# Folding two key chunks of one query tile per half head by a relu of their score difference

## The reference

```
q = x @ W_q + b_q;  k = x @ W_k + b_k;  v = x @ W_v + b_v
q = q @ W_s
scores = jnp.einsum('bhqd,bhkd->bhqk', q, k) / jnp.sqrt(jnp.float32(Hd))
attn = jax.nn.softmax(scores, axis=-1)
out = jnp.einsum('bhqk,bhkd->bhqd', attn, v)
```

## Time and profile before

| | |
|---|---|
| median of 3 runs | 1736.55 us (1734.66 to 1736.87) |
| profiled execution, its span | 1734.7 us |
| weighing in the attention loop, first to last start | 139.2 to 1397.7 us |
| PE, DVE, ACT, POOL busy | 97%, 87%, 74%, 13% |
| one unit in the steady loop | 19.64 us |

### The profile page before, as it was taken

How to read it: one execution, slowest core, us unless ns; L and a number is a source line. 1 busy time by engine, 2 the same in 40 slices (tenths; PEclk the granted TensorE clock), 3 DMA queues, 4 the chain that set the end, 5 groups by cost and what they waited for, 6 DMA issues and landing times. The chain is left out here.

```text
span 1734.7 us, 43731 instructions
## 1 busy us (share of the span) xinstructions
PE 1685.5 (97%) x17251; PEld 969.8 (56%) x17251; DVE 1513.5 (87%) x1908; ACT 1291.7 (74%) x2454; POOL 229.3 (13%) x300
## 2 busy tenths in 40 slices
PE   8999999999999999999999999999999998599998
PEld 5645555555555555555555554555555586488887
DVE  5678999999999999999999999999999476687774
ACT  2327888888888888888888888888888834365663
POOL 0422012100010000001000000100000012135433
PEclk9999999999999999999999999999999997599999
DMA  8660443222222223323222223342220331235332
GB/s 265 207 178 24 92 98 53 41 41 39 52 55 39 41 49 52 47 40 65 41 42 39 39 41 54 59 60 39 41 42 12 108 107 61 98 101 143 89 82 37
DMA packets 93658, 122.03 MB, mean 70 GB/s; under 512 B 24060, under 2 KB 70716, under 8 KB 90348
## 3 DMA queue, kind: packets, MB, share of 16 engines
q1 hardware_dynamic: 84492, 109.22, 28.1%
q0 software_dynamic: 6144, 8.39, 2.7%
q10 hardware_dynamic: 2816, 1.61, 0.3%
HBM read 79.35 MB, written 38.54 MB: 68 GB/s over the span
## 5 line engine op out<-in xcount | busy, mean ns | idle before, releaser
L230 DVE TENSOR_REDUCE pmax<-ps 128x2 f32<-128x1024 f32 x1024 | 1191.6, 1215 | 54.2 <-PE ps L223 50.2
L1080 ACT ACTIVATE pt<-ps 128x512 f32<-128x512 f32 x2048 | 1079.4, 600 | 179.8 <-PE ps L584 157.7
L223 PE MATMUL ps<-kp,qp 48*128 48x512 f32 x2048 | 622.4, 458 | 2.9 <-DVE pmax L230 2.9
L1139 PE MATMUL ps<-pt,v_st 128*32 128x256 f32 (+1 forms) x10752 | 589.7, 334 | 0.7 <-ACT pt L1080 0.7
L584 PE MATMUL ps<-qp,kp 50*128 50x512 f32 x2048 | 560.8, 422 | 0.5 <-ACT pt L1080 0.5
L584 PEld LDWEIGHTS ps<-qp,kp 50*128 50x128 f32 x2048 | 292.5, 185 | 265.2 <-ACT pt L1080 263.1
L1139 PEld LDWEIGHTS ps<-pt,v_st 128*32 128x32 f32 x10752 | 265.7, 109 | 261.0 <-issue 187.2
L223 PEld LDWEIGHTS ps<-kp,qp 48*128 48x128 f32 x2048 | 245.6, 184 | 108.1 <-issue 89.8
L213 POOL CAST m_parts<-rowmax_t 128x32 fp32r<-128x32 f32 x64 | 13.5, 211 | 864.5 <-DVE rowmax_t L247 864.5
L1752 PE MATMUL ps<-w_l,hid_h 128*128 128x256 f32 x256 | 72.3, 283 | 0.0
L446 ACT ACTIVATE pt<-ps,xb 128x512 fp32r<-128x512 f32 x32 | 21.8, 687 | 64.7 <-PE ps L613 63.7
(11 more groups left out here) (229 smaller groups left out, 1297.6 us busy)
## 6 DMA issues: line engine op xcount, KB each, us to landing
kp<-k_parts SPq DMA_DIRECT2D x186, 128.0 KB, 4.5
v_all<-L_ffn_w SPq DMA_DIRECT2D x16, 1024.0 KB, 6.9
qp<-q_parts SPq DMA_DIRECT2D x186, 64.0 KB, 4.1
k_parts<-pt SPq DMA_DIRECT2D x16, 512.0 KB, 3.4
q_parts<-pt SPq DMA_DIRECT2D x16, 512.0 KB, 2.9
o_rows<-o_sb SPq DMA_DIRECT2D x64, 128.0 KB, 3.4
sums_c<-o_rows SPq DMA_DIRECT2D x512, 0.5 KB
m_rows<-m_parts SPq DMA_DIRECT2D x256, 2.0 KB
```

Of the source, the lines that this page charges most:

```text
L223: last = nc.tensor.matmul(slot[:, half * CH:(half + 1) * CH], qp[rows, r, a * P:(a + 1) * P], kp[rows, r, c * CH:(c + 1) * CH], start=True ...
L230: v.reduce_max(pmax[:, u % 2, 2 * k:2 * k + 2], slot.rearrange("p (f t) -> p f t", f=2), AX.X).then_inc(groups_out, 1)
L1080: nc.scalar.activation(pt[:, s % PTS, half * CH:(half + 1) * CH], bank(n % SCORE_BANKS), ACT.Exp, scale=SCALE).then_inc(scores_out, 1)
L1139: last = mm(acc[32 * j:32 * (j + 1), first * QB:(first + many) * QB], v_st[:, h % NBUF, kt, :], probs[:, :, j * QB:(j + 1) * QB], start=kt ...
```

## The change

For 60 of the 64 units (2 to 61) two of the 16 groups are computed in another way. The fourth pair of tiles (FOLD_TILE = 3) has four key chunks; of those, 2 and 3 (groups k = 14 and 15) are folded: max(a, b) = b + relu(a - b).

- POOL makes a negated copy `q_minus` of the 128 queries (two operations, behind the split of the maxima of the unit before).
- PE computes q·k2 - q·k3 in the score ring, in the unit before, ahead of its chunk 6: for both halves one matmul with `qp` and then one with `q_minus` into the same bank. The two difference chunks take two successive places of the ring, so a unit now uses 34 of them.
- ACT takes the relu of both difference chunks from PSUM to `fold` (128 x 1024 in SBUF), between the exponentials of chunks 5 and 6.
- Group k = 14 is no longer filled or reduced. Group k = 15 is filled as before, and DVE adds `fold` to it and takes the maximum in one operation per half.
- One block per unit (b == 5, from unit 1 on) fills one group where it filled two. The order of the other groups and chunks stays.
- Counts on `scores_out`, `scores_full` and `groups_out` follow the new numbering.

The diff, cut to its core:

```diff
+FOLD_TILE, FOLD_FROM, FOLD_END = KT // NCH - 1, 2, UNITS - 2
+FOLD_K = FOLD_TILE * NCH + NCH - 1
+FOLD_PLACE = 6
+GROUPS = [(u, k) for u in range(UNITS) for k in range(KT) if not (folds(u) and k == FOLD_K - 1)]
+FOLD_BEFORE = {(u - 1) * UNIT_CHUNKS + FOLD_PLACE: u for u in range(FOLD_FROM, FOLD_END)}
+RING, FOLD_RING = [], {}
+for chunk in range(UNITS * UNIT_CHUNKS):
+    if chunk in FOLD_BEFORE:
+        for half in range(2):
+            FOLD_RING[FOLD_BEFORE[chunk], half] = len(RING) + len(FOLD_RING)
+    RING.append(len(RING) + len(FOLD_RING))
...
         def reduce_group(dve, v, n, slot):
-            u, k = divmod(n, KT)
+            u, k = GROUPS[n]
             dve.wait_ge(groups_full, n + 1)
-            v.reduce_max(pmax[:, u % 2, 2 * k:2 * k + 2], slot.rearrange("p (f t) -> p f t", f=2),
-                         AX.X).then_inc(groups_out, 1)
+            if folds(u) and k == FOLD_K:
+                if u < FOLD_FROM + 2:
+                    v.memset(pmax[:, u % 2, 2 * k - 2:2 * k], LOWEST)
+                for half in range(2):
+                    dve.wait_ge(scores_out, FOLD_RING[u, half] + 1)
+                    last = v.tensor_tensor_reduce(fold[:, half, :], slot[:, half * CH:(half + 1) * CH], fold[:, half, :],
+                                                  1.0, LOWEST, ALU.add, ALU.max,
+                                                  accum_out=pmax[:, u % 2, 2 * k + half:2 * k + half + 1])
+                last.then_inc(groups_out, 1)
+            else:
+                v.reduce_max(pmax[:, u % 2, 2 * k:2 * k + 2], slot.rearrange("p (f t) -> p f t", f=2),
+                             AX.X).then_inc(groups_out, 1)
...
+        def fold_scores(pe, u):
+            h, f = divmod(u, HALVES)
+            a = f * (QT // 2) + FOLD_TILE
+            pe.wait_ge(q_negated, u - FOLD_FROM + 1)
+            for half in range(2):
+                at, rows = FOLD_RING[u, half], slice(HALF * half, HALF * half + KROWS)
+                pe.wait_ge(scores_out, at - SCORE_BANKS + 1)
+                nc.tensor.matmul(ring_bank(at), qp[rows, h % NBUF, a * P:(a + 1) * P],
+                                 kp[rows, h % NBUF, 2 * CH:3 * CH], start=True, stop=False)
+            for half in range(2):
+                at, rows = FOLD_RING[u, half], slice(HALF * half, HALF * half + KROWS)
+                nc.tensor.matmul(ring_bank(at), q_minus[rows, :],
+                                 kp[rows, h % NBUF, 3 * CH:4 * CH], start=False, stop=True).then_inc(scores_full, 1)
+
+        def negate_queries(pool, g, u):
...
+            for half in range(2):
+                rows = slice(HALF * half, HALF * half + KROWS)
+                links["pool"](g.tensor_scalar(q_minus[rows, :], qp[rows, r, a * P:(a + 1) * P].bitcast(F32), -1.0, None, ALU.mult))
+            pool.sem_inc(q_negated, 1)
...
         def scores(pe, s, half):
...
-            if n >= SCORE_BANKS:
-                pe.wait_ge(scores_out, n - SCORE_BANKS + 1)
+            if at >= SCORE_BANKS:
+                pe.wait_ge(scores_out, at - SCORE_BANKS + 1)
...
+                def take_fold(u, half):
+                    act.wait_ge(scores_full, FOLD_RING[u, half] + 1)
+                    if u > FOLD_FROM:
+                        act.wait_ge(groups_out, GROUP_OF[u - 1, FOLD_K] + 1)
+                    nc.scalar.activation(fold[:, half, :], ring_bank(FOLD_RING[u, half]), ACT.Relu).then_inc(scores_out, 1)
...
+                    if b == BLOCKS // 2 and block > BLOCKS:
+                        twice = False
                     for n in range(many):
-                        if n == (0 if twice or b == DELAY else 1) and group < STEPS:
+                        if n == (0 if twice or b == DELAY else 1) and group < len(GROUPS):
                             next_group(group)
                             group += 1
+                        if chunk in FOLD_BEFORE:
+                            fold_scores(pe, FOLD_BEFORE[chunk])
                         scores(pe, *divmod(chunk, 2))
                         chunk += 1
```

More of the change, by code:

```diff
@@ L68, with folds @@
 GATHER_SPARE = 14
+LOWEST = -3.0e38
+FOLD_TILE, FOLD_FROM, FOLD_END = KT // NCH - 1, 2, UNITS - 2
+FOLD_K = FOLD_TILE * NCH + NCH - 1
+FOLD_PLACE = 6
+def folds(u):
+    return FOLD_FROM <= u < FOLD_END
+GROUPS = [(u, k) for u in range(UNITS) for k in range(KT) if not (folds(u) and k == FOLD_K - 1)]
+GROUP_OF = {at: n for n, at in enumerate(GROUPS)}
+FOLD_BEFORE = {(u - 1) * UNIT_CHUNKS + FOLD_PLACE: u for u in range(FOLD_FROM, FOLD_END)}
[5 more added lines that the diff above has]
+    RING.append(len(RING) + len(FOLD_RING))
 class Link:
@@ L569, in project_dve, with ring_bank @@
                     normalise(n + 2)
+        def ring_bank(at):
+            return bank(at % SCORE_BANKS)
+        def fold_scores(pe, u):
[12 more added lines that the diff above has]
+        def negate_queries(pool, g, u):
+            h, f = divmod(u, HALVES)
+            r, a = h % NBUF, f * (QT // 2) + FOLD_TILE
+            pool.wait_ge(operands_in[r], (h // NBUF + (r > 0)) * 16 * loads_of_head)
+            pool.wait_ge(parts_made, u)
+            if u > FOLD_FROM:
+                pool.wait_ge(scores_full, FOLD_RING[u - 1, 1] + 1)
+            for half in range(2):
+                rows = slice(HALF * half, HALF * half + KROWS)
+                links["pool"](g.tensor_scalar(q_minus[rows, :], qp[rows, r, a * P:(a + 1) * P].bitcast(F32), -1.0, None, ALU.mult))
+            pool.sem_inc(q_negated, 1)
         def scores(pe, s, half):
@@ L580, in scores @@
                 pe.wait_ge(low_done, chunks * 4 - 1)
-            if n >= SCORE_BANKS:
-                pe.wait_ge(scores_out, n - SCORE_BANKS + 1)
+            if at >= SCORE_BANKS:
+                pe.wait_ge(scores_out, at - SCORE_BANKS + 1)
             rows = slice(HALF * half, HALF * half + MROWS)
-            nc.tensor.matmul(bank(n % SCORE_BANKS), kp[rows, h % NBUF, kt * P:(kt + 1) * P],
+            nc.tensor.matmul(ring_bank(at), kp[rows, h % NBUF, kt * P:(kt + 1) * P],
                              qp[rows, h % NBUF, f * CH:(f + 1) * CH], start=True, stop=True).then_inc(scores_full, 1)
@@ L1044, in _ @@
                     split_maxima(pool, g, u)
+                    if folds(u + 1):
+                        negate_queries(pool, g, u + 1)
                     if 6 <= u < 6 + 2 * NB:
@@ L1066, in take_output @@
                     nc.scalar.copy(o_sb[:, u % 2, :], acc).then_inc(acc_out, 1)
+                def take_fold(u, half):
+                    act.wait_ge(scores_full, FOLD_RING[u, half] + 1)
+                    if u > FOLD_FROM:
+                        act.wait_ge(groups_out, GROUP_OF[u - 1, FOLD_K] + 1)
+                    nc.scalar.activation(fold[:, half, :], ring_bank(FOLD_RING[u, half]), ACT.Relu).then_inc(scores_out, 1)
                 for n in range(STEPS * 2):
+                    if n in FOLD_BEFORE:
+                        for half in range(2):
+                            take_fold(FOLD_BEFORE[n], half)
                     if n % UNIT_CHUNKS == BLOCK and n > UNIT_CHUNKS:
@@ L1078, in _ @@
                         act.wait_ge(pv_done, blocks_until(n - 2 * PTS))
-                    act.wait_ge(scores_full, n + 1)
-                    nc.scalar.activation(pt[:, s % PTS, half * CH:(half + 1) * CH], bank(n % SCORE_BANKS),
+                    act.wait_ge(scores_full, RING[n] + 1)
+                    nc.scalar.activation(pt[:, s % PTS, half * CH:(half + 1) * CH], ring_bank(RING[n]),
                                          ACT.Exp, scale=SCALE).then_inc(scores_out, 1)
@@ L1091, in invert @@
                     inverse(v, f).then_inc(inverse_made, 1)
-                for n in range(EARLY_GROUPS, STEPS):
-                    u, k = divmod(n, KT)
+                for n in range(EARLY_GROUPS, len(GROUPS)):
+                    u, k = GROUPS[n]
                     done = u - 3
@@ L1131, in weigh @@
                     ready = chunks_of(block)
-                    pe.wait_ge(scores_out, ready[-1] + 1)
+                    pe.wait_ge(scores_out, RING[ready[-1]] + 1)
                     for s in sorted({n // 2 for n in ready}):
@@ L1153, in _ @@
                     twice = b != DELAY and (b == 0 or b > DELAY and b % 2 == 1) or block == 2 * DELAY
+                    if b == BLOCKS // 2 and block > BLOCKS:
+                        twice = False
                     for n in range(many):
-                        if n == (0 if twice or b == DELAY else 1) and group < STEPS:
+                        if n == (0 if twice or b == DELAY else 1) and group < len(GROUPS):
                             next_group(group)
                             group += 1
+                        if chunk in FOLD_BEFORE:
+                            fold_scores(pe, FOLD_BEFORE[chunk])
                         scores(pe, *divmod(chunk, 2))
                         chunk += 1
-                    if twice and group < STEPS:
+                    if twice and group < len(GROUPS):
```

17 lines of the change are left out of this document (10 added, 7 removed).

## The result

| | before | after |
|---|---|---|
| median | 1736.01 us of 4 executions | 1801.17 us of 3 |
| profiled execution, span | 1734.7 us | 1799.4 us |
| weighing in the loop, first to last start | 139.2 to 1397.7 us | 139.4 to 1466.9 us |
| one steady unit | 19.64 us | 20.81 us |

The change makes the kernel slower: ratio 1.0382, 95% interval 1.0364 to 1.0401. The forecast was 1812 with a range from 1788 to 1835.

The account below looks back on a forecast made before the run. The prediction took PE's own sequence to bound the kernel, at 19.64 us per unit. Its terms, 1.50 - 0.24 = 1.26 us a unit times 60 = 75.6 us, added to the 1736.55 us median gave 1812 us, range 1788 to 1835.

Parts of the forecast that it names:

- PE's list sets the pace; relief of DVE is worth 0: In the attention loop, PE's own sequence sets 19.64 us per unit, so time saved on DVE gains 0.
- The slack: DVE's spare time in the steady loop, taken as some 0.7 us per unit.
- The two combined operations: On DVE, each 512-wide operation was taken as 0.691 us plus a 0.086 us accumulator read, 1.55 us for two.
- POOL, 0: Two negations on POOL behind the split of the maxima, used about 12 us later, cost 0.
- The dropped group, -0.24: In the unit's sixth block, one pair of 512-column matmuls fewer on PE gains 0.24 us a unit.
- The difference chunks, 0.48 of work and 1.02 of standing, +1.50: In PE's short block, added matmuls, then chunk 7 waiting for half 0's relu to free its bank: 1.50 us longer.
- the start of the relu: On ACT, half 0's relu was put 0.50 us after the second difference pair's start at 730.60, at 731.10.
- The sum: Over 60 units, 1.50 - 0.24 = 1.26 us each, 75.6 us in all, giving 1812 us.
- (a): Rival at the ring: PE hides the wait, only 0.24 us a unit counts, 1751 us, partly hidden up to 1800; chance 0.16.
- (b): Rival in the loop: DVE sets the pace, a unit shrinks by 0.7 us, 42 us in all, 1695 us; chance 0.05.
- (c): Rival on ACT: table loads between exponential and relu add 154 us, 1966 us; chance 0.03 with other ways of being slower.

Follow-up runs that it names:

- e1: Kernel before with group k = 14 left out in 60 units and nothing in its place; 1718.76 us, ratio 0.9907.
- e4: Kernel before plus one more DVE reduction of 512 elements per unit in 60 units; 1744.20 us, ratio 1.005.
- e5: Kernel before plus one more DVE reduction of 1024 elements per unit in 60 units; 1775.55 us, ratio 1.0263.
- e2: As e1, plus four matmuls of the difference's shape in the short block, written to the next group's slot, not the score ring; 1746.6 us, ratio 1.0079.
- e8: Changed kernel with both difference chunks ahead of chunk 8, in the next block, instead of chunk 6; 1813.07 us, ratio 1.0453.
- e3: Changed kernel with the relu over 64 of 512 columns and the combined operation writing its result back to PSUM; 1779.34 us, ratio 1.026.
- e9: Changed kernel with the difference chunks apart, half 0 ahead of chunk 6, half 1 ahead of chunk 8; 1812.34 us, ratio 1.0448.
- e7: Changed kernel with the short block reordered: chunk 6, the group, both difference chunks, chunk 7; 1777.62 us, ratio 1.025.
- e10: Changed kernel with each relu followed by a second one over 128 columns, which frees the bank; median of all four 2558.56 us.
- e6: Changed kernel with each full relu done twice, the second waiting for the first; 2739.02 us, ratio 1.5846.

## Why the prediction was right, step by step

**PE's list sets the pace; relief of DVE is worth 0.** Right. e1 took 1.2 us from DVE and gained 0.24; after took more and DVE's idle time grew to 2.6 us a unit, as forecast (2.7). The slack was 0.58 us rather than 0.7 (e4, e5). The two combined operations take 0.683 us each, against the 0.691 taken for them.

**POOL, 0.** Right. The two negations take 1.14 us together (732.19 to 733.33 us, used at 743.93) and end well ahead of their use; nobody waits for them.

**The dropped group, -0.24.** -0.24 in e1 alone, -0.27 in after.

**The difference chunks, 0.48 of work and 1.02 of standing, +1.50.** The mechanism was right, each step in its place; the measured sum is 1.43. Work alone is 0.47 (e2), the stand 0.94 (after less e2). The step that was mis-sized is the start of the relu. The prediction took 0.50 us from the matmul to ACT, from rows where ACT waits for a chunk of one matmul. Here ACT starts 0.44 us behind the second, accumulating pair (743.93 to 744.37; 0.42 in e8, 747.97 to 748.39). Why it starts sooner there no run shows. Counted from the group, the forecast had relu, chunk 7 and weighing at +1.09, +1.74 and +2.17; measured are +1.02, +1.67 and +2.10. From the relu on every step is exact: 0.595 for 0.600, release 0.05, weighing 0.43 behind chunk 7. e3 shows that the relu's length enters one for one.

**The sum.** 1.26 was forecast, 1.17 came: 60 x 0.09 = 5.4 us. With the one long unit of before (0.7) and the 4.5 us behind the loop that makes 10.6 of the 10.9 us by which the span of 1810.3 was missed. The 4.5 us were in no term: they are made behind the loop, by an operation of DVE's that was slow in before and, it seems, by two short dips of the granted clock behind it. All of that was in the trace of before; that it could go was not foreseen, and why it went is open. That operation took anything from 0.63 to 2.17 us in the profiles of all the kernels here (2.17 in e2, where no dip followed at this place, 1.09 in e9), so nothing ties it to the fold.

**The rivals.** (a) PE hides the wait: fell; 43 of 43 units stand. (b) DVE sets the pace: fell. (c) table loads: fell; each of the two kernels has five loads of 1.283 us, none of them between the loop's first and last exponential, and after has 120 relus of 0.595 us between those. The Trainium skill (ScalarE: Activation LUTs, section Table sets) has relu in every set, and the trace agrees for the set that is loaded here. A relu on VectorE was not tried.

## What to carry to other kernels

Ask of a saving first whether its engine sets the pace: a unit that happens to carry extra work, or an experiment that adds some, tells it better than busy shares in the loop of 96% (DVE) against 100% (PE, with modelled ends). A ring of three banks that is filled three chunks at a time has no place for a fourth between two weighings; whatever goes in there puts a whole pass of the consuming engine, start, pass and release, into the producer's list, about 1 us here, and moving it to another block moves the stand along (e8, e9). What made it smaller was an order in which the entry that must wait takes the bank that comes free earliest (e7, 0.40 us a unit). A ring of four banks was not tried. Work that is handed from the relieved engine to the pacing one must be priced with such a wait; 0.24 us saved and 1.41 us added is what the fold comes to.

## What the runs showed that I had not expected

The granted clock. In after it stays at the upper level, but one of its four executions took 2248.38 us at a mean clock of 0.75. In e10 all four lost it, and its profile shows the moment. The timeline of PE around the last short block at the upper level:

```profile
439.48 0.49 PE L646 MATMUL ps<-qp,kp 50*128 50x512 f32 x1 [0.73 <-ACT stage_b L1138]
439.90 1.46 PE L1214 MATMUL ps<-pt,v_st 128*32 128x256 f32 x16
441.29 0.79 PE L244 MATMUL ps<-kp,qp 48*128 48x512 f32 x2
```

PE stood 0.73 us for the relu, as it had 13 times before, once a unit, for 0.73 to 0.76 us, and right behind that stand the weighing takes 1.46 us instead of 0.86 and the group 0.79 instead of 0.50: the lower level. It holds until 2198 us, though PE is busy 98.86 of 100 us there; once a unit PE still stands for the relu, 0.57 us. In e6 the fall came at 186.5 us and lasted until 2340. So where 0.33 us more in a unit would cost 20 us, e10 took some 750 longer than after (2558.56 less 1801.17). With stands of 0.45 or 0.46 us of PE idle once a unit, after lost the clock in one of four executions and e8 and e9 in none of eight. Nor is it the relu alone that does it. The kernel e4 has none, and two of its six executions took 1774 and 1776 us. The profiled one shows a unit in which DVE waited 1.4 us for a transfer, and PE stood for DVE, 1.02 us and then 0.42:

```profile
1088.98 0.49 PE L225 MATMUL ps<-kp,qp 48*128 48x512 f32 x2 [1.02 <-DVE pmax L232]
```

At 1091.5 its clock fell, and 71.7 us later, in the same loop, it was back. In e6 and e10, where it did not come back, PE went on standing once a unit (0.89 and 0.57 us); in e4 no such stand followed. That is a contrast between three profiles and not a test. In the profile of e5 PE stood about 0.5 us for DVE in nearly every unit, and the clock stayed up through the loop. What decides in which unit it falls, and what brings it back, these runs don't settle.
